# Rotary attention: output products between the two sets of scores of a round, and three pairs of banks for the first group's row scores

## What is computed

```
q = (x @ wq + bq).reshape(b, s, 16, 16)
k = (x @ wk + bk).reshape(b, s, 2, 16)
v = (x @ wv + bv).reshape(b, s, 2, 16)
q = q * cos + rotate_half(q) * sin
q = q * hd ** (-0.5)
k = k * cos + rotate_half(k) * sin
k_exp = jnp.repeat(k, 8, axis=2); v_exp = jnp.repeat(v, 8, axis=2)
scores = jnp.einsum('bqhd,bkhd->bhqk', q, k_exp) * hd ** (-0.5)
attn = jax.nn.softmax(scores, axis=-1)
out = jnp.einsum('bhqk,bkhd->bqhd', attn, v_exp).reshape(b, s, d)
return out @ wo + bo
```

## Time and profile before

| | |
|---|---|
| time, median of 3 runs | 7398.05 us (7391.06 to 7411.15) |
| the profiled execution | 7394.19 us |
| its span | 7392.4 us |
| the rotary stage's groups, G = 0 to the tail | 650.84 us |
| mean granted clock of TensorE over the span | 0.913 of full speed |
| TensorE, VectorE, ScalarE, GpSimd busy | 87%, 53%, 37%, 33% of the span |

### The profile page before, as it was taken

How to read it: one execution, slowest core, us unless ns; L and a number is a source line. 1 busy time by engine, 2 the same in 40 slices (tenths; PEclk the granted TensorE clock), 3 DMA queues, 4 the chain that set the end, 5 groups by cost and what they waited for, 6 DMA issues and landing times. The chain is left out here.

```text
span 7392.4 us, 98146 instructions
## 1 busy us (share of the span) xinstructions
PE 6397.2 (87%) x36802; PEld 4566.4 (62%) x36802; DVE 3949.7 (53%) x6935; ACT 2731.4 (37%) x5574; POOL 2416.7 (33%) x2927
## 2 busy tenths in 40 slices
PE   5888888888888888888888888898999899999899
PEld 3666666666666666666656666654332466777666
DVE  5676666666766767666333333325653344444422
ACT  3444444444444344443234444431355212222211
POOL 3666566665665666656200000002000001111100
PEclk8888888888888888888899999998899899999999
DMA  0000000000000000000000000000000101121200
GB/s 25 4 4 4 1 4 4 4 4 4 1 4 4 4 4 4 4 1 1 13 10 10 7 12 10 7 20 6 1 1 1 46 16 61 66 71 66 82 5 8
DMA packets 39049, 111.56 MB, mean 15 GB/s; under 512 B 4352, under 2 KB 19968, under 8 KB 38656
## 3 DMA queue, kind: packets, MB, share of 16 engines
q1 hardware_dynamic: 38656, 106.21, 4.2%
HBM read 104.10 MB, written 2.10 MB: 14 GB/s over the span
## 5 line engine op out<-in xcount | busy, mean ns | idle before, releaser
L630 POOL TENSOR_TENSOR d_kq<-d_kq,d_tot 128x256 f32<-128x256 f32 x896 | 680.2, 779 | 1167.4 <-PE d_lpd L298 1157.4
L298 PE MATMUL d_lpd<-d_kq,d_kF 128*128 128x128 f32 x3584 | 550.8, 301 | 227.3 <-POOL d_tot L632 226.2
L704 DVE COPY_PREDICATED d_MA<-d_pairs,d_lpd 128x512 f32<-128x512 int32 x448 | 396.9, 886 | 469.7 <-PE d_lpd L298 467.2
L298 PEld LDWEIGHTS d_lpd<-d_kq,d_kF 128*128 128x128 f32 x3584 | 492.5, 212 | 242.9 <-POOL d_tot L632 241.5
L555 ACT ACTIVATE d_Xs<-d_xy 128x256 f32<-128x256 f32 x384 | 147.2, 383 | 1168.5 <-PE d_xy L394 1168.5
L394 PEld LDWEIGHTS d_xy<-d_Tm,d_MA 128*128 128x128 f32 x3072 | 445.3, 213 | 206.5 <-issue 193.9
L692 DVE SCALAR_TENSOR_TENSOR d_qkv<-d_raw,d_wts,d_qkv 128x512 f32<-128x512 f32 x576 | 543.3, 944 | 28.2 <-ACT d_qkv L506 14.5
L394 PE MATMUL d_xy<-d_Tm,d_MA 128*128 128x64 f32 x3072 | 440.7, 292 | 6.7 <-ACT d_TT L520 5.2
L976 POOL TENSOR_TENSOR f1rstd<-f1var,mhalf 128x4 f32<-128x4 f32 x4 | 4.0, 1007 | 1307.2 <-DVE f1var L1001 1307.2
L1563 DVE TENSOR_REDUCE r_nm<-r_rows 128x2 f32<-128x1024 f32 x256 | 302.5, 1219 | 195.2 <-PE r_rows L1418 194.8
L1426 PE MATMUL r_cols<-r_qT,r_kT 32*128 32x512 f32 x1024 | 361.7, 636 | 14.0 <-ACT r_pT L1499 12.8
(11 more groups left out here) (395 smaller groups left out, 14333.2 us busy)
## 6 DMA issues: line engine op xcount, KB each, us to landing
e_wts<-in_w3all SPq DMA_DIRECT2D x64, 897.0 KB, 4.5
d_wts<-in_headw SPq DMA_DIRECT2D x16, 583.5 KB, 3.7
f3ws<-in_f3w SPq DMA_DIRECT2D x17, 384.0 KB, 8.2
c_wq<-in_wq SPq DMA_DIRECT2D x16, 256.0 KB, 2.7
c_wo<-in_wo SPq DMA_DIRECT2D x16, 256.0 KB, 2.9
f2ws<-in_f2s SPq DMA_DIRECT2D x16, 256.0 KB, 6.4
f2qs<-in_f2q SPq DMA_DIRECT2D x16, 256.0 KB, 6.8
f1ws<-in_f1w SPq DMA_DIRECT2D x8, 384.0 KB, 6.0
```

Source lines behind the costliest of these rows:

```text
L298: last = nc.tensor.matmul(out[:, :, k], kF[:, u % 2, ch_(k)], moving[:, :, k, :, 1], start=True, stop=True)
L630: nc.gpsimd.tensor_tensor(v, v, bc(t_l[:, :, 0], 2, h), ALU.mult)
L704: nc.vector.copy_predicated(into, bc(mh(pairs[:, lv], h), 1, 2), lpd[:].rearrange("p (x m h) -> p x m h", x=2, h=h)).then_inc(masked, 1)
```

## The change

Three edits, all in `rotary_attention`.

1. The output products are issued at even steps from s = 4 on, where odd steps from s = 5 on had them. The round they belong to is the same. The order on TensorE was: even set, odd set, products; it is: even set, products, odd set. The finishing steps and the query transposes stay behind the odd set.
2. `rows_ps` and `cols_ps` become one tensor `ps` of seven banks. In G = 0 the row sets take three pairs in turn (banks 0 and 1, 2 and 3, 4 and 5); the transposes of queries in G = 0 all use bank 6. Elsewhere row sets use the pairs at 0 and 2, and column uses banks 4 to 6 in turn, as before.
3. The waits follow: each use waits until the last use of the same bank or pair is read. Behind G = 0 TensorE also waits until all row sets are read.

```
-        rows_ps = c.enter_context(nc.psum_tensor("r_rows", [P, 2, 2, GRP], F32))
-        cols_ps = c.enter_context(nc.psum_tensor("r_cols", [P, 3, GRP], F32))
+        ps = c.enter_context(nc.psum_tensor("r_ps", [P, 7, GRP], F32))
...
+        FIRST_ROWS = NT + STEPS
+        col_bank, col_before = [], []
+
+        def add_cols(bank):
+            before = max([u for u, k in enumerate(col_bank) if k == bank], default=None)
+            col_bank.append(bank)
+            col_before.append(before)
+
+        def row_pair(use):
+            if NT <= use < FIRST_ROWS:
+                return 2 * ((use - NT) % 3)
+            return 2 * (use % 2)
+
+        def row_before(use):
+            return max((u for u in range(use) if row_pair(u) == row_pair(use)), default=None)
...
+        for use in range(slot):
+            add_cols(6 if 2 * NT <= use < 2 * NT + 4 else 4 + use % 3)
...
                 def into_cols():
                     nonlocal col
-                    if col >= 3:
-                        pe.wait_ge(cols_read, col - 2)
+                    if col_before[col] is not None:
+                        pe.wait_ge(cols_read, col_before[col] + 1)
                     col += 1
-                    return (col - 1) % 3
+                    return col_bank[col - 1]
 
                 def into_rows():
                     nonlocal row
-                    if row >= 2:
-                        pe.wait_ge(rows_read, row - 1)
+                    if row_before(row) is not None:
+                        pe.wait_ge(rows_read, row_before(row) + 1)
                     row += 1
-                    return (row - 1) % 2
+                    return row_pair(row - 1)
...
-                        if G and s % 2 == 1 and s >= 5:
+                        if G and s % 2 == 0 and s >= 4:
                             outputs(G - 1, s // 2 - 2)
...
                     if G < 4:
                         pe.wait_ge(cols_read, col)
+                    if G == 0:
+                        pe.wait_ge(rows_read, row)
...
-                            nc.vector.tensor_reduce(nm[:, t % 2, half, 4 * j + i0:4 * j + i0 + 2], rows_ps[:, (row - 1) % 2], AX, ALU.max).then_inc(rows_read, 1)
+                            nc.vector.tensor_reduce(nm[:, t % 2, half, 4 * j + i0:4 * j + i0 + 2], ps[:, row_pair(row - 1):row_pair(row - 1) + 2], AX, ALU.max).then_inc(rows_read, 1)
```

More of the change, by code:

```diff
@@ L1357, in heads_transposed @@
                     for j in range(4):
-                        last = nc.tensor.transpose(cols_ps[:, k, j * P:(j + 1) * P], qp[:, t, 4 * j:4 * j + 4].rearrange("p h d -> p (h d)"), T.ident[:])
+                        last = nc.tensor.transpose(ps[:, k, j * P:(j + 1) * P], qp[:, t, 4 * j:4 * j + 4].rearrange("p h d -> p (h d)"), T.ident[:])
                     last.then_inc(cols_mm, 1)
@@ L1363, in keys_transposed @@
                     for g in range(G2):
-                        last = nc.tensor.transpose(cols_ps[:, k, g * P:(g + 1) * P], kp[:, t % 4, g].rearrange("p h d -> p (h d)"), T.ident[:])
+                        last = nc.tensor.transpose(ps[:, k, g * P:(g + 1) * P], kp[:, t % 4, g].rearrange("p h d -> p (h d)"), T.ident[:])
                     last.then_inc(cols_mm, 1)
@@ L1370, in _ @@
                         for kd in range(KD):
-                            last = nc.tensor.matmul(rows_ps[:, r, 0, 0:W], T.xnT[:, kd, tok(t)], wqkv[:, kd], start=(kd == 0), stop=(kd == KD - 1))
+                            last = nc.tensor.matmul(ps[:, r, 0:W], T.xnT[:, kd, tok(t)], wqkv[:, kd], start=(kd == 0), stop=(kd == KD - 1))
                         last.then_inc(rows_mm, 1)
@@ L1394, in finish @@
                         for j in range(4):
-                            last = nc.tensor.transpose(cols_ps[:, k, j * P:(j + 1) * P], oT[:, (t // 4) % 2, j, (t % 4) * P:(t % 4 + 1) * P], T.ident[:])
+                            last = nc.tensor.transpose(ps[:, k, j * P:(j + 1) * P], oT[:, (t // 4) % 2, j, (t % 4) * P:(t % 4 + 1) * P], T.ident[:])
                         last.then_inc(cols_mm, 1)
@@ L1400, in finish @@
                         for kd in range(KD):
-                            last = nc.tensor.transpose(cols_ps[:, k, kd * P:(kd + 1) * P], oall[:, t % 2, kd * P:(kd + 1) * P], T.ident[:])
+                            last = nc.tensor.transpose(ps[:, k, kd * P:(kd + 1) * P], oall[:, t % 2, kd * P:(kd + 1) * P], T.ident[:])
                         last.then_inc(cols_mm, 1)
@@ L1406, in finish @@
                         for kd in range(KD):
-                            last = nc.tensor.matmul(cols_ps[:, k, 0:D], oallT[:, t % 2, kd], wo[:, kd], start=(kd == 0), stop=(kd == KD - 1))
+                            last = nc.tensor.matmul(ps[:, k, 0:D], oallT[:, t % 2, kd], wo[:, kd], start=(kd == 0), stop=(kd == KD - 1))
                         last.then_inc(cols_mm, 1)
@@ L1417, in _ @@
                                 keys = slice((t // QT) * S + half * GRP, (t // QT) * S + (half + 1) * GRP)
-                                last = nc.tensor.matmul(rows_ps[:, r, w, :], qT[band(i0 + w), j, tok(t)], kT[band(i0 + w), j // 2, keys], start=True, stop=True,
+                                last = nc.tensor.matmul(ps[:, r + w, :], qT[band(i0 + w), j, tok(t)], kT[band(i0 + w), j // 2, keys], start=True, stop=True,
                                                         tile_position=((i0 + w) * PAD, 0))
@@ L1425, in _ @@
                                 k = into_cols()
-                                nc.tensor.matmul(cols_ps[:, k, :], kT[band(i), jj // 2, tok(b * QT + kt)], qT[band(i), jj, (G - 1) * GRP:G * GRP], start=True, stop=True,
+                                nc.tensor.matmul(ps[:, k, :], kT[band(i), jj // 2, tok(b * QT + kt)], qT[band(i), jj, (G - 1) * GRP:G * GRP], start=True, stop=True,
                                                  tile_position=(i * PAD, 0)).then_inc(cols_mm, 1)
@@ L1487, in finish @@
                             act.wait_ge(added, t - 1)
[L1488 removed]
+                        nc.scalar.activation(ys[:, t % 2, :], ps[:, k, 0:D], ACT.Copy).then_inc(cols_read, 1)
                 for G in range(5):
```

15 lines of the change are left out of this document (7 added, 8 removed).

## The result

The changed kernel takes 7426.9 us (median of 8 runs, 7416.84 to 7438.74), the kernel before 7411.42 us beside it (8 runs, 7391.06 to 7416.98): a ratio of 1.0034, 95% interval 1.0021 to 1.0047. It is slower, since the interval leaves out 1. Whether it is slower by more than the 0.3% set above is not settled: the interval reaches from 0.21% to 0.47%, and the quotient of the two medians is 1.0021. The profiled execution took 7416.84 us, 22.65 more than the profiled one of before.

The account below looks back on a forecast made before the run. The first group was taken as bound by waiting on two bank pairs, later groups by latency through three column banks, not engine work. 7394.2 - 32.5 + 12 + 27 + 4 = 7404.7, say 7405 us; range 7373 to 7424.

Parts of the forecast that it names:

- Part 1: First group, G = 0: a third bank pair removes VectorE's wait, giving 80.0 us, a gain of 32.5 us.
- Part 2: Plain rounds after the first group: moving the products only shifts the stall between sets; the round stays 3.87 us.
- Part 3: Products starting a head group wait for ScalarE's output bank copy: twelve waits of 1.24 us, 10.1 us after giving back 0.4 each.
- Part 4: Ends of groups: last transposes wait for row maxima, 5 us, less 0.7 back four times at group starts; net 2 us.
- The drain at a change of tiling mode: Some 40 moved steps might each cost one more TensorE drain, about 4 us, left inside the bounds.
- Part 5: TensorE's clock falls at three new waits in G = 4, +27 us (bounds +3, +56); longer low stretch in G = 1, +4.
- 0.48 per us at half: Cost of half clock in G = 4, from one fall: 1.63 us lost in 3.41 us.
- The base: Whole kernel before the change: the sum started from its profiled execution of 7394.2 us, 4 under the median of 7398.05.
- B: Rival: the clock holds in G = 4 but for short dips, giving 7379 us; chance 0.25.
- C: Rival: the wait for the output bank copy is mostly hidden, so the clock holds too, 7367 us; chance 0.08.
- D: Rival: in G = 4 the clock, once down, stays down; 7434 us at 120 us of half clock; chance 0.12.
- A: The forecast itself for the whole kernel, 7390 to 7424 us; chance 0.55.

Follow-up runs that it names:

- pairs only: Changed kernel with the output products put back at odd steps, keeping the three pairs; 7376.91 us against 7396.26 for the kernel before, ratio 0.9975.
- the filler: 128 unused matmuls added in G = 4 to each kernel: changed one 7376.37 us against 7396.26, ratio 0.9973; kernel before 7391.64 against 7409.56, ratio 0.9982.
- the copy first: Changed kernel with ScalarE's copy of the output bank issued ahead of its step's two exponentials; 7352.7 us, ratio 0.9946 to the kernel before.
- the order alone: Kernel before with only the output products moved between the even and odd sets; 7444.71 us, ratio 1.0072.
- the second profile: Kernel before, unchanged, profiled once more on another chip; 7413.83 us.
- the version with seven banks: Changed kernel with the output bank's copy ahead of the exponentials and column uses in G = 4 taking seven banks in turn; 7318.84 us, ratio 0.9878.

## Why the prediction was wrong

Forecast was "within 0.3%" at 7405 us, with a range of 7373 to 7424. It came to 7426.9 and slower by 0.34%: the range was missed by 3 us. Step by step, between the two first profiles:

- **Part 1, three pairs: right.** G0 80.0 forecast, 82.3 measured, a gain of 30.2 for 32.5, inside the bounds; the reads 1.13 apart. In pairs only, with the clock up earlier, 33.6. The waits behind the transposes (1.83, 1.64, 1.07) are 4.5 us where I took 2 in all: that is about the 2.3 missing.
- **Part 2, the stall only moves: right.** A plain round is still 3.87.
- **Part 3, the copy's wait: right.** Twelve waits of 1.27 for 1.24 forecast. The 0.4 given back after each wasn't there: 1.32 a wait on the path in G3.
- **Part 4, ends of groups: about right in sum, not in its parts.** The transposes at G1's end do wait for VectorE, 1.58 us:

```profile
5341.54 0.19 DVE L1584 TENSOR_REDUCE r_qp<-r_nm 128x16 f32<-128x32 f32 x1
5341.79 0.66 PE L1374 MATMUL r_ps<-ident,r_qp 128*128 128x128 f32 x4 [1.58 <-DVE r_qp L1584]
```

  but a whole group of the new order without the copy's wait is 1.2 us shorter than before, so more comes back than I counted. With the filler in both kernels and 0.40 us taken off per us of extra half clock (an estimate: the price was measured in G4), the order costs 7.2 - 2.8 in G1, 3.8 - 1.4 in G2, 2.8 in G3 and 3.7 - 1.4 in G4: 11.9 us, where parts 2 to 4 said 12. That parts of it cancel is luck.
- **The drain at a change of tiling mode.** The Trainium skill, "TensorEngine Tiling (Array Packing)", Key Properties, says that changing the tiling mode drains the engine. My estimate of about 4 us for it stood beside the sum. No run shows such a cost: with the copy first, G2 and G3 in the new order are shorter than before.
- **Part 5, the clock: the mechanism right, its size wrong.** This is the step that failed: "Three falls of 20.5 us are 61 us at half". There were two falls at copy waits in G4, not three, and they lasted 37.6 and 47.8 us: 88.7 at half in one execution. It was 116.1 in the other, 75.1 at a copy wait and 41.0 without one, and 95.6 with the order alone. I had carried one length over from G0, a group with other work, though the earlier trace rows show a longer one beside it (65.7 us); and 20.5 is the length of the stretch that I printed, while the clock rose only at 5229.8, 23.9 us after it fell. Why a fall lasts as long as it does in G4 no run shows. My price of 0.48 per us at half was too high, 0.40 to 0.41 measured in four pairs: I had read it from a fall of 3.41 us with TensorE busy for all of it, while a round holds a stall of 0.67 us that is no longer at half clock. The two errors partly cancel: 85.3 more us at 0.40 are 34, not 27. G1's clock came at 13.5 us at half for 3.7: +3.9, forecast +4. G2's 6.8 us at half, +2.7, I hadn't counted.

The sum with the measured terms is -30.2 + 11.9 + 34.4 + 3.9 + 2.7 = +22.7, and the profiled executions differ by 22.65. As the terms are differences of these profiles, that they add up tests nothing but the bookkeeping. Forecast was +10.5.

- **The base: the larger part of the miss in the time itself.** "The profiled execution took 7394.2 us, 4 under the median of 7398.05". Of 8 runs beside the changed kernel the median of before was 7411.42. I took an execution in which G4 kept its clock for the kernel; it has another in which G4 loses 17 us. The rows for this stood in the profile (a fall at 5649.65 and a quick rise), and I priced what the change does to it, not what before does without it. Of the 22.2 us between 7404.7 and 7426.9, 17.2 are the base (7411.42 - 7394.2) and 5.0 the change (+15.5 between medians, +10.5 forecast). That it is +15.5 and not +22.7 fits a kernel before that loses in G4 too in most of its runs. Its granted clocks say the same: of the 17 runs beside the filler the eight above 7410 us have a mean clock of 0.910 or 0.911, the four below 7393 have 0.914. Over a span of 7400 us a difference of 0.003 is 44 us at half clock, by my estimate, about the length of the fall in the second profile. Only one such execution was profiled, so this is inferred.

Of the rivals, B and C fall (the waits are exposed, the clock fell). D, "in G4 the clock, once down, stays down", is nearer to the truth than A: its bound of 92 us at half for over 7420 lies between the two measured times, but its "stays down" is too strong, since the clock rose at 5700.5. I gave it 0.12; the one fall already in the trace, of a kernel without the new wait, should have made it more.

The Trainium skill, "TensorE: Matmul & The Clock Gate", "A second HAM failure mode: psum-queue depth-cycling", says that cycling through PSUM banks with small idle times can make the clock fall and cost throughput. I wrote that the trace agrees only in part. In G4 the runs agree with it that the clock falls and that a fall costs time, 0.40 us per us at half. What starts and ends one they don't settle: with the same ring of three and its 0.67 us a round the kernel before was at half for 3.4 us in one execution and 44.4 in another, the changed kernel with the copy first not at all, and no run separates the stall from the four sets without products at G4's start.

## What to carry to other kernels

When a kernel's granted clock falls even once in some stage, a single profile of it is one draw: take two or three before adding up terms, and give the time at half clock a range of its own. When steps move past each other on one engine, look at what the other engine issues in the same step: here moving a 0.6 us copy two instructions earlier on ScalarE turned +0.34% into -0.54%, each against the kernel before. And where a round's stall moves but doesn't shrink when its parts are reordered, count the buffers of its ring: seven banks instead of three in one group gave more than all reordering.

## What was not expected of the hardware

- Waits of 1.27 us bring short falls of 3.4 us in G1 and G2 (16 at the 36 waits of G1 to G3 in four profiles, none in the seven profiles without them), and long ones in G4 (37.6 to 95.6 us); waits of 1.74 us in the version with seven banks bring none.
- Two executions of one program differ by 17 us in one stage by the clock alone: 3.4 us or 44.4 us at half in G4 of the kernel before.
- 128 unused matmuls in G4 make both kernels faster: the changed one goes from +0.34% to -0.27% against the kernel before, that one itself gains 0.18%, and its spread narrows from 32.8 us (17 runs, 7389.0 to 7421.8) to 8.2 (12 runs, 7388.72 to 7396.93).
- Half the clock costs 0.40 to 0.41 of the time spent at it in this stage, not half: the stall of a round, 0.67 us, is as long at either clock.
